# Rotary tables moved to VectorE, scores handled bank by bank, feed-forward residual and statistics earlier in VectorE's order

## The reference

```
attention:  16 heads of 8 columns, per-head Wq, Wk, Wv (8 x 8), causal softmax over 1024 positions,
            out = P V, concatenated, scrambled (transpose and reshape), @ W_O
stack, 6 layers:
  x = local_attention(shift(x)) + x
      qkv = x @ Wqkv                     (128 x 3072), 16 heads of 64
      q, k = l2norm(q) * q_scale, l2norm(k) * k_scale
      q = q*cos*scale + rotate_half(q)*sin*scale ; k the same with 1/scale
      softmax over the window of 32 and the window before it, P V, @ Wo
  x = ffn(x) + x
      xn = LayerNorm(x) * ln_g + ln_b ; a, gate = split(xn @ W1 + b1)    (341 columns each)
      (a * gelu(gate)) @ W2 + b2
```

## Time and profile before

| | us |
|---|---|
| median of 3 runs | 2115.48 |
| lowest and highest | 2111.0 and 2120.15 |
| the profiled execution, its own time | 2128.67 |
| its span, first to last instruction | 2126.9 |
| TensorE busy | 1940.5 (91%) |
| VectorE busy | 1658.7 (78%) |
| GpSimd busy | 1418.3 (67%) |
| ScalarE busy | 1305.8 (61%) |
| mean granted clock of TensorE | 0.953 of full |

### The profile page before, as it was taken

How to read it: one execution, slowest core, us unless ns; L and a number is a source line. 1 busy time by engine, 2 the same in 40 slices (tenths; PEclk the granted TensorE clock), 3 DMA queues, 4 the chain that set the end, 5 groups by cost and what they waited for, 6 DMA issues and landing times.

```text
span 2126.9 us, 74573 instructions
## 1 busy us (share of the span) xinstructions
PE 1940.5 (91%) x33032; PEld 1322.8 (62%) x33032; DVE 1658.7 (78%) x1635; ACT 1305.8 (61%) x1547; POOL 1418.3 (67%) x1403
## 2 busy tenths in 40 slices
PE   3989899589999999999899998899999999999985
PEld 1434444357767666776677776667767676676774
DVE  5765562489888888889888988887888888988862
ACT  1355457356667766667666765666776666766752
POOL 1000000699988898879888888597889887888820
PEclk7799999789999999999999999999999999999997
DMA  3141100033233333333223323233333333322221
GB/s 103 39 133 46 44 25 12 28 82 77 70 86 75 87 71 77 90 78 85 63 65 87 91 71 90 49 79 86 74 86 72 79 93 74 72 63 66 69 67 45
DMA packets 144033, 151.51 MB, mean 71 GB/s; under 512 B 60760, under 2 KB 85596, under 8 KB 142944
## 3 DMA queue, kind: packets, MB, share of 16 engines
q1 hardware_dynamic: 143712, 146.75, 27.5%
HBM read 35.75 MB, written 5.44 MB: 19 GB/s over the span
## 4 chain that ended last, share of the span: by engine, by line
PE 32%; DVE 22%; POOL 21%; issue 15%; SPq 5%; ACT 3%; DMA 1%; POOLq 0%; DVEq 0%; ACTq 0%
POOL arena L1109 8%; POOL arena L1117 5%; SPq L1273 4%; DVE arena L626 4%; PE banks L408 4%; DVE ss L713 3%; PE banks L471 3%; PE banks L538 3%; PE banks L480 3%; DVE mx_t L748 3%; PE banks L565 3%; PE banks L391 2%; PE banks L498 2%; DVE arena L721 2%; PE banks L511 2%
## 5 line engine op out<-in xcount | busy, mean ns | idle before, releaser
L1109 POOL TENSOR_TENSOR arena<-arena,tab_sl 128x512 f32<-128x512 f32 x384 | 589.2, 1565 | 16.2 <-ACT arena L917 9.9
L1117 POOL TENSOR_TENSOR arena<-arena 128x1024 f32<-128x1024 f32 x192 | 488.0, 2563 | 0.0
L721 DVE TENSOR_TENSOR arena<-arena,rn 128x1024 f32<-128x1024 f32 x192 | 359.9, 1915 | 113.9 <-POOL rn L1085 113.9
L471 PE MATMUL banks<-w_qkv,arena 128*128 128x512 f32 x768 | 358.4, 609 | 8.3 <-ACT arena L909 5.5
L946 ACT ACTIVATE arena<-arena 128x1024 f32<-128x1024 f32 x96 | 101.6, 1058 | 407.9 <-DVE arena L752 407.9
L626 DVE TENSOR_REDUCE arena<-banks 128x1 f32<-128x1024 f32 (+7 forms) x176 | 175.1, 1027 | 105.1 <-PE banks L372 104.8
L538 PE MATMUL banks<-arena 64*64 64x32 f32 x12288 | 244.0, 222 | 4.0 <-DVE arena L752 3.4
L538 PEld LDWEIGHTS banks<-arena 64*64 64x64 f32 x12288 | 233.2, 135 | 16.9 <-DVE arena L752 5.3
L480 PE MATMUL banks<-ident,arena 128*128 128x128 f32 x1536 | 208.1, 291 | 33.9 <-DVE arena L762 18.5
L471 PEld LDWEIGHTS banks<-w_qkv,arena 128*128 128x128 f32 x768 | 139.4, 191 | 160.0 <-issue 150.8
L762 DVE TENSOR_TENSOR arena<-banks,tab_cl 128x1024 f32<-128x1024 f32 x192 | 226.2, 1219 | 11.8 <-ACT arena L917 10.2
(11 more groups left out here) (108 smaller groups left out, 3067.8 us busy)
## 6 DMA issues: line engine op xcount, KB each, us to landing
arena<-arena SPq DMA_DIRECT2D x1512, 64.0 KB
arena<-parts_dram SPq DMA_DIRECT2D x64, 144.0 KB
w_qkv<-Wqkv SPq DMA_DIRECT2D x6, 1024.0 KB
parts_dram<-arena SPq DMA_DIRECT2D x12, 256.0 KB, 3.1
tab_cl<-tab_c SPq DMA_DIRECT2D x6, 512.0 KB, 7.3
tab_sl<-tab_s SPq DMA_DIRECT2D x6, 512.0 KB
w_o<-Wo SPq DMA_DIRECT2D x6, 512.0 KB
w_qkv<-Wqkv SPq DMA_DIRECT2D x6, 512.0 KB, 4.6
```

The source lines that it names most:

```text
L471: last = e.matmul(ps[:, BANK * c:BANK * (c + 1)], xsT[b][:, P * t:P * (t + 1)], w_qkv[:, at:at + BANK], start=True, stop=True)
L721: e.tensor_tensor(to, to, rn[n // 2 % 2][:, n % 2, HEADS * m:HEADS * (m + 1)].unsqueeze(2).to_broadcast([P, HEADS, HEAD_DIM]), ALU.mult).t ...
L1109: e.tensor_tensor(qk_sw[:, m, :].rearrange("p (h d) -> p h d", d=HEAD_DIM)[:, :, d:d + HALF], raw[:, m, :].rearrange("p (h d) -> p h d", d ...
L1117: e.tensor_tensor(to, to, qk_sw[:, m, :], ALU.add).then_inc(S["rs"], 1)
```

## The change

- Scores by banks: each unit's scores and transposed scores are signalled, read and released one bank (512 columns) at a time. There are two maxima and two exponentials a unit; a head with over 512 columns gets two partial maxima, which `a_maxima_split` joins with one more operation on VectorE.
- The tables of layers 1 to 5 are multiplied by VectorE, the cosines at the end of turn 10 of the layer before, the sines at the end of turn 14 (both are turns k = 0); GpSimd no longer does it. The tables of layer 0 stay on GpSimd.
- `ff_residual(G - 1)` comes ahead of `subtract` in k = 1.
- `ff_stats(G)` moves from the end of k = 1 to the end of k = 0, and `ff_rsqrt(G)` on GpSimd from k = 2 to k = 1.

```diff
+        def pieces(j, many, n, bank):
+            if many == 1:
+                return slice(j, j + 1), BANK * bank, min(n, BANK * (bank + 1))
+            return slice(j + bank * many // 2, j + (bank + 1) * many // 2), 0, n
...
-        def place(use, n_pairs, *readers):
+        def place(use, n_pairs, *readers, by_bank=False):
...
-            last_on[i] = [readers[k:k + 2] for k in range(0, len(readers), 2)]
+            whole = [readers[k:k + 2] for k in range(0, len(readers), 2)]
+            first = [(done, count - 1) for done, count in whole] if by_bank else whole
+            last_on[i] = (first, whole)
...
             def a_scores(k):
...
-                ps = pair("a_sc", k)
...
+                for bank in range(2):
+                    heads, c0, c1 = pieces(j0, many, n, bank)
+                    ps = pair("a_sc", k, bank=bank)
+                    for j in range(heads.start, heads.stop):
...
+                    last.then_inc(S["a_sc"], 1)
...
             def a_maximum(k):
...
+                for bank in range(2):
+                    heads, c0, c1 = pieces(j0, many, n, bank)
+                    to = m_first[g % 2][:, qt - tiles // 2, heads] if c1 < n else m_neg[g % 2][:, qt, heads]
+                    w.wait_ge(S["a_sc"], 2 * k + bank + 1)
+                    e.tensor_reduce(to, banks[:, pair_of["a_sc", k], BANK * bank:BANK * (bank + 1)].rearrange(
...
             def a_maxima_split(g):
...
+                upper = m_neg[g % 2][:, tiles // 2:tiles, :]
+                e.tensor_tensor(upper, upper, m_first[g % 2], ALU.min).then_inc(S["a_mstep"], 1)
...
+            def scale_cos(l):
...
+                tab = tab_cl[l % 2][:, :, :, :]
+                e.tensor_tensor(tab, tab, qk_gain[:, :, :].unsqueeze(1).to_broadcast([P, tiles, 2, HEAD_DIM]), ALU.mult).then_inc(S["tab_c"], 1)
...
+            def scale_sin(l):
...
+                for d, o in ((0, HALF), (HALF, 0)):
+                    tab = tab_sl[l % 2][:, :, :, d:d + HALF]
...
...
+                if s >= FF and k == 1 and G > 0:
+                    ff_residual(G - 1)
                 if 0 <= s - 4 < n_tiles:
                     subtract(s - 4)
-                if s >= FF and k == 1 and G > 0:
-                    ff_residual(G - 1)
...
-                if ff_here and k == 1:
+                if ff_here and k == 0:
                     ff_stats(G)
+                if s % all_tiles == 10 and s // all_tiles + 1 < layers:
+                    scale_cos(s // all_tiles + 1)
+                if s % all_tiles == 14 and s // all_tiles + 1 < layers:
+                    scale_sin(s // all_tiles + 1)
...
...
-                if s % all_tiles == 7 and s // all_tiles + 1 < layers:
-                    scale_cos(s // all_tiles + 1)
-                if s % all_tiles == 9 and s // all_tiles + 1 < layers:
-                    scale_sin(s // all_tiles + 1)
...
-                if s >= FF and k == 2 and G < n_groups:
+                if s >= FF and k == 1 and G < n_groups:
                     ff_rsqrt(G)
```

More of the change, by code:

```diff
@@ L330, in tensor_program, with pair @@
             w = Once(e)
-            def pair(*use):
-                for done, count in before[use] or []:
-                    w.wait_ge(S[done], count)
+            def pair(*use, bank=1):
+                if before[use]:
+                    for done, count in before[use][bank]:
+                        w.wait_ge(S[done], count)
                 return banks[:, pair_of[use], :]
@@ L362, in a_scores @@
                 n = P * (qt + 1)
-                ps = pair("a_sc", k)
                 w.wait_ge(S["masks_b"], 1)
[L365 to L373, removed]
+                for bank in range(2):
+                    heads, c0, c1 = pieces(j0, many, n, bank)
+                    ps = pair("a_sc", k, bank=bank)
+                    for j in range(heads.start, heads.stop):
+                        slot, at = slot_of(g, j), apart * (j - j0)
+                        w.wait_ge(stack_in[slot], STACK_DMAS * 16 * (g // 3 + 1))
+                        last = e.matmul(ps[:, at + c0:at + c1], QS[slot][0:ROWS, P * qt:P * (qt + 1)],
+                                        KS[slot][0:ROWS, c0:c1], start=True, stop=True)
+                        if c1 == n:
+                            last = e.matmul(ps[:, at + n - P:at + n], ident_b, mask_rows, start=False, stop=True, skip_group_check=True)
+                    last.then_inc(S["a_sc"], 1)
             def a_maxima_out(g):
@@ L383, in a_weigh @@
                 q0, n = P * kt, seq - P * kt
-                ps = pair("a_wsc", s)
                 w.wait_ge(S["ones_out"], 16 * RING)
[L386 to L394, removed]
+                for bank in range(2):
+                    heads, c0, c1 = pieces(j0, many, n, bank)
+                    ps = pair("a_wsc", s, bank=bank)
+                    for j in range(heads.start, heads.stop):
+                        slot, at = slot_of(g, j), apart * (j - j0)
+                        w.wait_ge(rows_in[slot], 16 * (g // 3 + 1))
+                        last = e.matmul(ps[:, at + c0:at + c1], KS[slot][0:ROWS + PARTS, q0:q0 + P],
+                                        QS[slot][0:ROWS + PARTS, q0 + c0:q0 + c1], start=True, stop=True)
+                        if c0 == 0:
+                            last = e.matmul(ps[:, at:at + P], ident_b, mask_cols, start=False, stop=True, skip_group_check=True)
+                    last.then_inc(S["a_wsc"], 1)
             def a_gather(g, kt):
@@ L622, in a_maximum @@
                 n = P * (qt + 1)
-                w.wait_ge(S["a_sc"], k + 1)
                 if g >= 2:
                     w.wait_ge(S["a_mlo"], g - 1)
-                e.tensor_reduce(m_neg[g % 2][:, qt, j0:j0 + many],
-                                banks[:, pair_of["a_sc", k], :].rearrange("p (j n) -> p j n", j=many)[:, :, 0:n],
-                                AX_X, ALU.max, negate=True).then_inc(S["a_max"], 1)
+                for bank in range(2):
+                    heads, c0, c1 = pieces(j0, many, n, bank)
+                    to = m_first[g % 2][:, qt - tiles // 2, heads] if c1 < n else m_neg[g % 2][:, qt, heads]
+                    w.wait_ge(S["a_sc"], 2 * k + bank + 1)
+                    e.tensor_reduce(to, banks[:, pair_of["a_sc", k], BANK * bank:BANK * (bank + 1)].rearrange(
+                        "p (j n) -> p j n", j=heads.stop - heads.start)[:, :, 0:c1 - c0], AX_X, ALU.max, negate=True).then_inc(S["a_max"], 1)
             def a_maxima_split(g):
@@ L865, in a_exp @@
                 n, quad = seq - P * kt, g * tiles + kt
-                w.wait_ge(S["a_wsc"], s + 1)
                 w.wait_ge(S["a_gather"], max(0, quad - 1))
-                e.activation(pt_ring[quad % 2][:, j0:j0 + many, 0:n],
-                             banks[:, pair_of["a_wsc", s], :].rearrange("p (j n) -> p j n", j=many)[:, :, 0:n], ACT.Exp,
-                             scale=float(A_DIM) ** -0.5).then_inc(S["a_exp"], 1)
+                for bank in range(2):
+                    heads, c0, c1 = pieces(j0, many, n, bank)
+                    w.wait_ge(S["a_wsc"], 2 * s + bank + 1)
+                    e.activation(pt_ring[quad % 2][:, heads, c0:c1],
+                                 banks[:, pair_of["a_wsc", s], BANK * bank:BANK * (bank + 1)].rearrange(
+                                     "p (j n) -> p j n", j=heads.stop - heads.start)[:, :, 0:c1 - c0], ACT.Exp,
+                                 scale=float(A_DIM) ** -0.5).then_inc(S["a_exp"], 1)
             def a_copy_sums(g):
```

30 lines of the change are left out of this document (20 added, 10 removed).

## The result

| | before | after |
|---|---|---|
| median, us | 2113.24 (4 runs, 2108.25 to 2120.15) | 2186.42 (4 runs, 2178.73 to 2192.93) |
| profiled execution, its span | 2128.67, 2126.9 | 2183.63, 2181.8 |
| mean granted clock | 0.953 | 0.938 |

The change makes the kernel slower: 1.0343 times the time before, 95% interval 1.0295 to 1.039, or +73 us. Forecast were +27 to the median, 2142 us, in a range of 2070 to 2180. On another chip it was 1.045 (1.0407 to 1.0492). The direction and the main mechanism, a wait for the transfers of shift_rows, are those of the prediction; the size is not, and neither is its reason for the late transfer. In the profile's chain of work that ended last, SyncE's queue and the DMA have 21% and 12%, where they had 5% and 1% before.

A forecast was written before the change was run, and what follows sets the result against it. Bound: TensorE in k = 3 and k = 0, VectorE from the scores of k = 1 to L741 of k = 2. Terms +43 - 2 - 23 + 25 - 21 = +22, plus 5 on the median 2115.5: 2142 us, range 2070 to 2180.

The forecast's parts named there:

- late transfers and drain: Second stage: statistics in k = 0 wait for shift_rows, 2.0 us a group, +43 (+8 to +78); drain's norm earlier, -2.
- the tables off GpSimd: Table turns of five layers: three L741 of 8.12 to 11.44 us vanish, -23; 5 us less counted against the median.
- Tables on VectorE: End of k = 0: table multiplications stand between landing and scaling, 5.1 us a layer, +25 (+12 to +45).
- Scores by banks: First stage: 3.0 us of TensorE's waiting gone in 7.7 groups, less 2, -21 (-45 to +5).
- Start of the statistics behind the maxima of k = 0: VectorE in k = 0 starts statistics when shift_rows' data lands, 1.6 us behind the issue's end, at 1164.7 and 1234.6.
- Start of the statistics to the maxima of k = 1: VectorE from landing: statistics, two scalings at 4.0 us, then residual; maxima come 4.4 and 4.7 us late.
- Maxima of k = 1 to L759 of k = 2: VectorE's stretch, without statistics and residual, takes 24.9 us in place of 27.5.
- TensorE waits about 1 us for the residual: Second stage, k = 1: TensorE's L548 output matmuls wait for VectorE's residual by about 1 us.
- What would show it: Signs: VectorE gap of 3 to 8 us in k = 0, k = 1 of 18 us, no L741 over 5, score groups of 36.
- The transfers are no wait: Rival: shift_rows lands early enough for the statistics in k = 0; 2041 us; chance 0.17 (no wait or small).
- The port lock: Rival: VectorE's two-input work beside GpSimd's rotation waits, +40, 2182 us; chance 0.13 with a costlier cut.
- the small third transfer: SyncE's queue in k = 0: shift_rows' third transfer, L1285, itself takes 6.52 us, so the data lands late.

The follow-up runs named there:

- e3_banks_only: Kernel before with scores, transposed scores, maxima and exponentials by banks alone; 2085.0 us, 0.9895.
- e8_residual_only: Kernel before with the residual ahead of subtract in k = 1 alone; 2103.72 us, 0.997.
- e2_stats_up: Kernel before with the statistics at the end of k = 0 and ff_rsqrt in k = 1 alone; 2246.64 us, 1.0668.
- e9_stats_and_residual: Kernel before with statistics at the end of k = 0, ff_rsqrt in k = 1 and residual ahead of subtract; 2196.94 us, 1.0423.
- e10_tables_back: Changed kernel with the tables of layers 1 to 5 back on GpSimd; 2172.86 us, 1.0312.
- e11_even_tables_back: Changed kernel with shift_rows' 127-partition transfer cut in 112 and 15 and the tables back on GpSimd; 2038.55 us, 0.968.
- e5_even_shift: Changed kernel with shift_rows' 127-partition transfer cut in one of 112 partitions and one of 15; 2062.61 us, 0.9779.
- e14_changed_again: Changed kernel, unaltered, run again on the chip of `e13_wait_filled`; 2202.19 us, 1.045.
- e7_tables_only: Kernel before with the tables of layers 1 to 5 scaled by VectorE at the end of turns 10 and 14 alone; 2111.11 us, 1.0009.
- e13_wait_filled: Changed kernel with the four projection matmuls of each k = 1 turn done twice; 2179.79 us, 1.0357.
- e4_rows_apart: Changed kernel with shift_rows' third transfer, three runs of 64 values, cut in three transfers; 2212.7 us, 1.051.

## Why the prediction came out as it did

The forecast was +27: +41 for late transfers and drain, -18 for the tables off GpSimd against the median, +25 for them on VectorE, -21 for the scores. Measured are +89 to +92, 0, +7 to +29 and -22. The step that failed is the first, by some 50 us: the forecast took the start of the statistics from two groups (15.4 us behind the maxima of k = 0, measured 16.5 over all), held the stretch from there to the end of k = 2 to be free of any fall of the clock, and took the drain for a gain (-2, measured +10). The second failed too, by 18.

*Scores by banks, -21:* right in sum, -22 alone, with some luck in the working. For the group of the earlier trace rows 3.0 us were forecast and 6.0 came, its clock at 1.00 in place of 0.91, which was counted in the bound alone. Over the eight groups the maxima take 274.2 us in `e3_banks_only` and 298.7 before, 3.1 a group, and 270.8 in the changed kernel.

*Tables off GpSimd, -23:* failed. Two of the three long L741 come back at the same places in `e3_banks_only` (8.43 and 8.22 us), the third, of 11.44, doesn't. `e8_residual_only` has one, of 7.44, in another layer. In `e2_stats_up`, `e9_stats_and_residual`, `e10_tables_back` and `e11_even_tables_back` GpSimd scales the tables and no such row exists. They come and go with the order of other instructions: by the prediction's 5 us for each of the two that recur, an estimate, they are worth some 10 us in the order before and nothing in the changed one. I had priced a collision as if it belonged to the operation. Nor does the L741 at 1032.44 span six GpSimd instructions, as I had read it: it begins in the second of the four L1109 and so meets five. What holds it so long stays open.

*Tables on VectorE, +25:* the operations cost what was forecast, 5.5 us a layer in the changed kernel's trace (cosines 1.5, the pair of sines 4.1, on average) for 5.1. In time it is 21 to 24 us between `e5_even_shift` and `e11_even_tables_back`. Between the changed kernel and `e10_tables_back` it is 7 us by the ratio of the first chip, 1.0343, whose interval overlaps that of `e10_tables_back`, and 29 by the ratio of `e14_changed_again`, 1.045. In the kernel before, `e7_tables_only` gives 0: slack hides part, and the long rows go.

*Late transfers and drain, +43 - 2:* the step that carries the miss. Statistics and residual alone (`e9_stats_and_residual`) give +89 to +92. By its own terms, from the timelines of groups 0 to 21 of the changed kernel:

- Start of the statistics behind the maxima of k = 0: forecast 14.5 and 16.2, mean 15.4; measured 16.5 on average, 14.1 to 21.0. Group 0 has it at 21.0 and the groups in turn 6 of a layer at 16.3 to 20.7, because the queue comes to shift_rows later there. The trace before shows that (L1285 ends 13.1 to 16.9 us behind the maxima in the groups in turn 6, against 12.9 in that of the earlier trace rows); I took two groups for all 22. Landing is 2.1 us behind the issue's end in place of 1.6. Together 1.2 us a group, some 26 us.
- Start of the statistics to the maxima of k = 1: forecast 6.7 and 1.1 for the tables; measured 7.5. Right.
- Maxima of k = 1 to L759 of k = 2: forecast 24.9; measured 25.1 in most groups, 27.1 to 27.4 in three where the clock stayed low, mean 25.5: 14 us.
- Drain: -2 forecast; from the maxima of group 21 to the end 142.8 us after, 132.9 before, +10. The statistics wait for the transfers here too.

26 + 14 + 12 on top of 41 are 93, against the 89 to 92 of `e9_stats_and_residual`. In that run's own trace the three are 12, 16 and 11, so that 80 are explained and some 10 are not. The parts add: -22 and +89 are 67, and `e10_tables_back`, which has both, shows 67. The tables' 7 to 29 us on top of it are the difference to the kernel itself, 73 us on the first chip and 97 on the other, and so no test of the sum.

*TensorE waits about 1 us for the residual:* it waits 3.8 us on average (79.4 by 21). With that came the clock, whose fall the prediction put at nothing without a reason: 116 us of the k = 1 turns pass at 1.2 GHz in the changed kernel's trace, some 20 in that of before. That the fall costs time is shown by `e13_wait_filled`; that it makes the difference between 1.034 and 1.045 (3 turns of 17 us in the first trace, 9 in the second) is likely, not shown.

*What would show it.* No L759 over 5 us, and VectorE's gap ended by a DMA: seen, though gaps reach 11.2 us. Score groups of 36 us: that of the earlier trace rows has 33.0. Counted by the projections as the earlier trace rows, group 13 has k = 1 of 21.6 us where 18 were forecast, and k = 2 of 14.5 where 14.2 were.

*Rivals.* "The transfers are no wait" (2041 us) describes `e5_even_shift`, 2063 with the tables' 24 us in it, and 2039 without them. The port lock did not decide: the pair L798 takes 3.84 us in group 13 in place of 1.4, and the pair L739 takes over 5 us in 32 places, up to 6.6, where the pair L721 did in 3 before, but no row of 8 us appears, and the stretch from the statistics to the maxima came out at the forecast's length.

The cause that the prediction gave for the late landing, the small third transfer, was wrong, and this mattered for what to do next. The Trainium skill, page DMA: Bandwidth & Descriptors, section "Why a DMA increments its semaphore by 16 and not by 1", says that a transfer is spread over the largest number of engines up to 16 that divides the outermost dimension of both its sides, so that 127 partitions go to one engine. The trace agrees: share 0.08 and 18 GB/s while L1321 moves, and 0.94 and 214 GB/s where its two halves, of 112 and 15 partitions, move together with the rest of L1320. It would not have changed the forecast of this change, whose landing came from the rows either way.

What stays open: whether cutting the small transfer in `e4_rows_apart` costs anything. Against the first run of the changed kernel it is 26 us slower, but against `e14_changed_again` 10, with intervals that overlap (1.0453 to 1.0566, and 1.0407 to 1.0492), and from the maxima of group 0 to those of group 21 the two traces differ by 1 us. Open too is what makes the clock stay low for 9 to 13 us in some k = 1 turns and for 5 or less in others of the same kernel.

## What to carry to other kernels

A wait at the head of VectorE's queue costs what stands behind it, and TensorE, starved by this, came back here at half its clock: follow the wait to TensorE, and see whether it goes idle. Before you price a wait on a transfer, look at its landing in every group of the loop, not in two, and compare bytes with rate: a rate of one engine's share points to the transfer's shape. The shift by one partition was better moved as 112 and 15 partitions than as 127.

## What the hardware showed that I had not expected

- A transfer of 127 partitions by four runs of 64 values moves at 18 GB/s for 7 us and more; as 112 and 15 partitions the pair is through in some 2 to 3 us, in which the DMA reaches 214 GB/s together with the rest of L1320.
- The time is charged, in the queue's rows, to the transfer behind it: 6.96 us for one that takes 0.75 otherwise.
- In a wait of 4.46 us of TensorE its granted clock fell to 1.2 GHz, and the first matmuls behind it took 3.78 us in place of 1.95.
- VectorE's two L739 take 2.4 us in group 13, 3.3 beside GpSimd's short products, and 5.4 to 6.6 where GpSimd's sums L1158 run beside them; a sum takes 2.4 us, and 3.3 where it falls on an L739.
